# Modulated convolution chain, four layers on one core: the prologue in another order on PE, ACT and DVE

## The reference

```python
def _layer(x, style, w, b, mw, mb, typ):
    s = style @ mw.T + mb
    weight = SCALE * w * s[:, None, :, None]
    demod = lax.rsqrt(jnp.sum(weight * weight, axis=(2, 3)) + EPS)
    weight = weight * demod[:, :, None, None]
    if typ == 'same':
        out = jax.vmap(_conv_same)(x, weight) + b[None, :, None]
    elif typ == 'upsample':
        out = jax.vmap(_conv_up)(x, weight.transpose(0, 2, 1, 3)) + b[None, :, None]
        out = _blur(out, 2.0 * blur_k, (1, 1))
    elif typ == 'downsample':
        xb = _blur(x, blur_k, (2, 2))
        out = jax.vmap(_conv_down)(xb, weight) + b[None, :, None]
    return out
# TYPES = ('same', 'upsample', 'same', 'downsample'); result = x + layer3(layer2(layer1(layer0(x))))
```

## Time and profile before

| | us |
|---|---|
| timed runs: median (lowest to highest of 3) | 169.01 (168.2 to 170.15) |
| the profiled execution's own time | 168.33 |
| its span | 166.5 |
| PE busy in the span | 158.8 (95%) |
| DVE busy | 131.8 (79%) |
| POOL busy | 94.4 (57%) |
| ACT busy | 56.4 (34%) |

### The profile page before, as it was taken

The page is one execution under the profiler, slowest core; times in us unless marked ns, Lnnn a source line. Parts: engine busy times, 40 slices in busy tenths (PEclk is TensorE's granted clock), DMA queues, the critical chain, the costliest instruction groups (busy, mean ns, idle before and its releaser), DMA issues. The chain is left out here.

```text
span 166.5 us, 8946 instructions
## 1 busy us (share of the span) xinstructions
PE 158.8 (95%) x3975; PEld 146.1 (88%) x3975; DVE 131.8 (79%) x229; ACT 56.4 (34%) x127; POOL 94.4 (57%) x155
## 2 busy tenths in 40 slices
PE   7999999999999999999999999999999999999970
PEld 5687888959789789999899999999999999999960
DVE  7859877788868869778696969696979797969993
ACT  3245561323142332334251514243434334231120
POOL 7209908596493977456373829191919192837530
PEclk9959999999999999999999999999999999999998
DMA  4982000120302204335343445353634242030314
GB/s 119 274 212 14 2 4 4 55 79 4 125 8 65 68 4 126 130 130 190 105 183 118 182 133 186 129 193 111 213 110 145 88 143 101 7 126 4 132 74 180
DMA packets 13990, 17.81 MB, mean 107 GB/s; under 512 B 5216, under 2 KB 5760, under 8 KB 13952
## 3 DMA queue, kind: packets, MB, share of 16 engines
q1 hardware_dynamic: 13888, 17.22, 31.1%
q10 hardware_dynamic: 64, 0.02, 0.1%
HBM read 8.85 MB, written 8.39 MB: 104 GB/s over the span
## 5 line engine op out<-in xcount | busy, mean ns | idle before, releaser
L190 POOL TENSOR_TENSOR Hw<-Hw 128x192 f32<-128x192 f32 x15 | 9.0, 598 | 50.8 <-DVE Hw L885 50.8
L546 PE MATMUL p_m<-uu,Hw 64*64 64x128 f32 x992 | 31.6, 269 | 0.0
L546 PEld LDWEIGHTS p_m<-uu,Hw 64*64 64x64 f32 x992 | 29.4, 132 | 0.1
L466 PE MATMUL p_lo<-xin,w0s 64*64 64x259 f32 x384 | 27.7, 406 | 0.1
L309 POOL COPY Hw<-Hw 64x896 f32<-64x896 f32 x15 | 25.8, 1722 | 1.0
L466 PE MATMUL p_le<-xin,w0s 64*64 64x260 f32 x384 | 26.3, 389 | 0.0
L511 PE MATMUL p_le<-R_sb,F_st 64*64 64x128 f32 (+2 forms) x768 | 25.8, 266 | 0.3 <-issue 0.3
L536 PE MATMUL p_m<-u,Hw 64*64 64x256 f32 x384 | 25.4, 375 | 0.0
L896 DVE TENSOR_TENSOR uu<-u 128x516 f32<-128x516 f32 x32 | 24.3, 796 | 1.4
L911 DVE TENSOR_TENSOR e_sb<-p_lo,s_sb 128x512 f32<-128x512 f32 x16 | 11.1, 696 | 16.8 <-PE p_lo L546 16.6
L511 PEld LDWEIGHTS p_le<-R_sb,F_st 64*64 64x64 f32 x768 | 23.3, 133 | 1.1 <-issue 0.9
(11 more groups left out here) (140 smaller groups left out, 217.8 us busy)
## 6 DMA issues: line engine op xcount, KB each, us to landing
xin<-in_x_dram SPq DMA_DIRECT2D x32, 256.0 KB, 3.3
out_dram<-ot SPq DMA_DIRECT2D x32, 256.0 KB, 2.4
wn<-in_L_cond_weights_dram SPq DMA_DIRECT2D x1, 192.0 KB, 3.5
mwn<-in_L_cond_mod_w_dram SPq DMA_DIRECT2D x1, 128.0 KB, 2.2
xe<-in_x_dram SPq DMA_DIRECT2D x2, 56.0 KB, 7.7
cn<-in_cond_dram ACTq DMA_DIRECT2D x1, 16.0 KB, 2.0
bn<-in_L_cond_mod_b_dram ACTq DMA_DIRECT2D x1, 1.0 KB
bn<-in_L_cond_biases_dram ACTq DMA_DIRECT2D x1, 1.0 KB
```

Of the source, the lines that this page charges most:

```text
L466: ins = pe.matmul(bank[h * C:(h + 1) * C, s, 0:n], w0s[p % 2][rows, k, :], xin[p % NX][rows, i0:i0 + 2 * n - 1:2], start=(k == 0), stop=(k ...
L546: ins = pe.matmul(bank(h)[s * C:(s + 1) * C], tap(p, h, s, blk), moving(slice(h * C, (h + 1) * C), s, k), start=(k == 0), stop=(k == len(b ...
```

## The change

The warm-up of PE and its tile are removed. Layer 0 of pair 0 is started as soon as its scaled weights are there; the transposes of wsum stand after its first tap, in p_le instead of p_lo, and the demodulation matmuls after its second.

The diff, cut to its core:

```diff
@@ PE @@
-            pe.wait_ge(warm_made, 1)
-            for _ in range(4):
-                pe.matmul(p_le[:, 1, 0:256], pe_warm[:, 0:P], pe_warm[:], start=True, stop=True)
...
-            layer0_odd(0)
+            pe.wait_ge(w0s_made, 1)
+            pe.wait_ge(x_loaded[0], 32)
+            layer0(0, p_lo, NO, 1, lo_done, [0])
+            pe.wait_ge(made["wsum"], 1)
+            for l in range(LAYERS):
+                ins = pe.transpose(p_le[0:C, 0, l * C:(l + 1) * C], wsum[:, l, :], ident[0:C, 0:C])
+            ins.then_inc(put["wsumT"], 1)
+            layer0(0, p_lo, NO, 1, lo_done, [1])
+            pe.wait_ge(copied["wsumT"], 1)
+            pe.wait_ge(made["style2"], 1)
...
+            ins.then_inc(put["demod"], 1)
+            layer0(0, p_lo, NO, 1, lo_done, [2])
             layer0(0, p_le, NE, 0, le_done)
-            pe.wait_ge(copied["V_st"], 2)
-            compose_R(0)
...
             blurred_taps(1, p_m2[:, 1], cid2, NF).then_inc(put["FT"], 1)
+            pe.wait_ge(copied["V_st"], 2)
+            compose_R(0)
+            pe.wait_ge(copied["G_mv"], 1)
+            blurred_taps(3, b_m13[1], cid1, 3).then_inc(put["oT"], 1)
+            pe.wait_ge(copied["F_st"], 1)
+            compose_H(0)
             taps_transposed(2, b_m13[0], 256).then_inc(put["w2T"], 1)
+            compose_R(1)
...
-            compose_H(0)
-            compose_R(1)
-            blurred_taps(3, b_m13[1], cid1, 3).then_inc(put["oT"], 1)
@@ ACT @@
-            act.wait_ge(put["wsumT"], 1)
-            copy(wsumT[:], p_lo[0:C, 0, 0:LAYERS * C].rearrange("p (l c) -> p l c", c=C), copied["wsumT"])
...
             copy_both(G_mv, p_m13[0:C, 1, 0, 0:K * C].rearrange("p (a c) -> p a c", c=C), copied["G_mv"])
+            act.wait_ge(put["wsumT"], 1)
+            copy(wsumT[:], p_le[0:C, 0, 0:LAYERS * C].rearrange("p (l c) -> p l c", c=C), copied["wsumT"])
...
+            evac_odd(0)
             act.wait_ge(made["e2"], 1)
...
             make_A(0)
-            evac_odd(0)
-            act.wait_ge(made["e1"], 1)
-            evac_R(0)
             act.wait_ge(put["FT"], 1)
...
+            act.wait_ge(made["e1"], 1)
+            evac_R(0)
             make_A(1)
...
@@ DVE @@
-            dve.memset(pe_warm[:], 0.0).then_inc(warm_made, 1)
...
-            then()
-            step(dve.tensor_reduce(wsum[:], wsq[:], AX_X, ALU.add), "wsum")
...
-            tt(style2[:], style[0:C], style[0:C], ALU.mult, "style2")
             ts(pvec[0:C, W_S0], style[0:C, 0, 0:B:2], 1.0)
             ts(pvec[C:P, W_S0], style[C:P, 0, 1:B:2], 1.0, name="s0")
+            step(dve.tensor_reduce(wsum[:], wsq[:], AX_X, ALU.add), "wsum")
+            tt(style2[:], style[0:C], style[0:C], ALU.mult, "style2")
...
+            make_diffs(0)
             demodulation(0, 2)
-            make_diffs(0)
...
-            make_uu(0)
-            demodulation(3, 4)
...
+            demodulation(3, 4)
...
             edge_x0()
+            make_uu(0)
             dve.wait_ge(put["oc"], 1)
```

More of the change, by code:

```diff
@@ L87, in modulated_conv_kernel @@
         sqrt_warm = sb("sqrt_warm", [P, 1])
-        pe_warm = sb("pe_warm", [P, 256])
         y_st = sb("y_st", [P, 6, C])
@@ L130, in modulated_conv_kernel @@
         padded = sem("padded")
-        warm_made = sem("warm_made")
         zeroed = sem("zeroed")
@@ L440, in _ @@
             taps_transposed(0, b_m13[0], 0).then_inc(put["w0T"], 1)
[L442 to L445, removed]
             for a in range(K):
@@ L450, in _, with layer0 @@
             ins.then_inc(put["GT"], 1)
[L452 to L461, removed]
+            def layer0(p, bank, n, first, done, ks=range(K)):
+                for k in ks:
                     for s in range(2):
@@ L468, in layer0 @@
                                             stop=(k == K - 1), skip_group_check=True)
-                ins.then_inc(done, 1)
+                if ks[-1] == K - 1:
+                    ins.then_inc(done, 1)
             def layer0_odd(p):
@@ L629, in edge_out @@
                 ins.then_inc(put["oe"], 1)
-            layer0_odd(0)
+            pe.wait_ge(w0s_made, 1)
[8 more added lines that the diff above has]
+            pe.wait_ge(made["style2"], 1)
+            for l in range(LAYERS):
+                ins = pe.matmul(p_m2[0:C, 0, 256 + l * B:256 + (l + 1) * B], wsumT[:, l], style2[:, l, :],
+                                start=True, stop=True)
+            ins.then_inc(put["demod"], 1)
+            layer0(0, p_lo, NO, 1, lo_done, [2])
             layer0(0, p_le, NE, 0, le_done)
-            pe.wait_ge(copied["V_st"], 2)
-            compose_R(0)
             pe.wait_ge(made["cid"], 1)
@@ L645, in _ @@
             ins.then_inc(put["yc"], 1)
-            pe.wait_ge(copied["F_st"], 1)
-            compose_H(0)
-            compose_R(1)
-            blurred_taps(3, b_m13[1], cid1, 3).then_inc(put["oT"], 1)
             layer0_odd(1)
@@ L772, in _ @@
                            scale=1.0 / 32).then_inc(copied["F_st"], 1)
+            act.wait_ge(made["e1"], 1)
+            evac_R(0)
             make_A(1)
-            act.wait_ge(put["w2T"], 1)
-            copy(w2T[:], p_m13[0:C, 0, 1, 0:3 * C].rearrange("p (k c) -> p k c", c=C), copied["w2T"])
+            act.wait_ge(put["oT"], 1)
+            act.activation(o_st[:], p_m13[:, 1, 0, 0:3 * C].rearrange("p (a c) -> p a c", c=C), ACT.Copy,
+                           scale=0.125).then_inc(copied["o_st"], 1)
             scale_w0(1)
@@ L778, in _ @@
             evac_H(0)
+            act.wait_ge(put["w2T"], 1)
+            copy(w2T[:], p_m13[0:C, 0, 1, 0:3 * C].rearrange("p (k c) -> p k c", c=C), copied["w2T"])
             evac_R(1)
             make_A(2)
-            act.wait_ge(put["oT"], 1)
-            act.activation(o_st[:], p_m13[:, 1, 0, 0:3 * C].rearrange("p (a c) -> p a c", c=C), ACT.Copy,
-                           scale=0.125).then_inc(copied["o_st"], 1)
             evac_odd(1)
```

## The result

| | before | after |
|---|---|---|
| timed runs: median, us (lowest to highest of 20) | 168.6 (167.95 to 170.15) | 170.62 (169.06 to 172.32) |
| the profiled execution's own time, us | 168.33 | 169.27 |
| its span, us | 166.5 | 167.5 |

The changed kernel is slower: ratio 1.0089, 95% interval 1.0061 to 1.0118. (It compares means, 168.75 with 170.26, and leaves out as disturbed three of the 20 runs after, 171.79 to 172.32; with them it would be 1.0105.) The forecast was 169.1, with 167.5 to 170.6 as the range.

The account below looks back on a forecast made before the run. PE was taken to bound the main loop (busy 39.65 of 40 us), so prologue shifts move the end: 168.33 + 0.92 (demodulation) - 0.70 (POOL) + 0.55 (w2) = 169.1 us. The range was 167.5 to 170.6.

Parts of the forecast that it names:

- the mark that I summed for: Start of layer 0 of pair 1 on PE, where the prologue releases the main loop: 21.24 instead of 20.47, +0.77 us.
- the first of the signs that I had set for being wrong: Forecast counts as wrong if PE doesn't wait for POOL inside compose_H(0), where about 1 us was expected.
- Warm-up away: Prologue: saves 3.78 us of PE with little to do; style at 5.9 to 6.5; 0.2 added for lower clock.
- The demodulation late: PE prologue: demodulation, behind wsum's transposes and two layer 0 taps, starts at 9.56 against 8.64, +0.92 us.
- The clock back at 11.9: PE's granted clock rises at 11.9 as before, so layer 0's even half mostly runs at the higher level.
- POOL decides: POOL's chain from e2 shortens by 0.7 to 5.42 us; F's copy ends at 18.48; PE waits about 1.0 us.
- w2 costs 0.55: w2's transposes ahead of compose_R(1) on PE delay R_sb and layer 0 of pair 1 by 0.55 us.
- DVE's other moves cost nothing: Moved differences, demodulation(3,4) (1.0 us, before zc) and uu(0) (1.38 us, behind edge_x0) cost no time.
- A: The case as summed: layer 0 starts early, the demodulation late, POOL's chain ends last; 169.1 us, chance 0.45.
- B: Faster: clock comes back during layer 0's first tap, near 8.5; 167.5 us, chance 0.2.
- C: Slower: clock low for another stretch, with PE waiting before the last third of compose_H(0); 170.7 us, chance 0.15.
- D: Slower on DVE: uu(0)'s two operations each wait for a POOL copy of place_H(1); 170.2 us, chance 0.1.

Follow-up runs that it names:

- b_nowarm: Kernel before without the four PE warm-up matmuls and their tile, order otherwise untouched: 166.92 us, ratio 0.9916 to before.
- a_warm: Changed kernel with the four warm-up matmuls and their tile put back: 171.59 us, ratio 1.0169 to before.
- a_head: Changed kernel with layer 0 whole behind the demodulation, and demodulation(3,4), w2's transposes and the first steps in old order: 167.21 us, ratio 0.9917 to before.
- a_poolfree: Changed kernel without POOL's wait for e2 ahead of prod: 170.56 us, ratio 1.0134 to before.
- b_uu: Kernel before with make_uu(0) moved behind edge_x0 on DVE: 168.08 us, ratio 0.9987 to before.
- a_w2_d34: Changed kernel with demodulation(3,4) back ahead of the first block sum and w2's transposes and copy back at their old places: 168.56 us, ratio 1.0014 to before.
- b_nowarm_uu: Kernel before without the warm-up and with make_uu(0) behind edge_x0: 167.11 us, ratio 0.9925 to before.
- a_nosplit: Changed kernel with layer 0 of pair 0 in one piece behind wsum's transposes and the demodulation: 171.12 us, ratio 1.0122 to before.

## Why the prediction was right or wrong

The direction of the change at the mark that I summed for, and the end, were right: layer 0 of pair 1 at 21.46 against 21.24, the profiled time 169.27 against 169.1, and the loss within 1%. But the median, 170.62, lies at the upper end of my range, and the loss of 0.89%, 1.5 us, is about twice the 0.77 us that I forecast. The way there was right only in part, and it failed at the first of the signs that I had set for being wrong: PE doesn't wait for POOL inside compose_H(0). That 21.24 came close is luck. PE reached compose_H(0) at 17.96, 1.7 later than my 16.3: 0.9 of it is the even half at the lower level, 0.5 the demodulation and the taps around it. That took the place of the wait of 1.0 for POOL, which isn't there, and of 0.3 that I gave w2 too much.

- **Warm-up away.** style at 5.9 to 6.5 held (5.96 to 6.56), and layer 0's early start nearly (7.75 against 7.45). What failed is the judgement of the edit as a whole: it is a gain of 0.84%, and so hides that the rest of the change costs twice what the result shows. I never summed what the edit does alone. The 0.2 for the lower level was also too small: the groups of 0.65 and 0.74 take 1.06 and 0.90. The Trainium skill (TensorE: Matmul & The Clock Gate, "Why this matters for your kernels") names warming up with matmuls first as the way to benchmark matmul accurately. It doesn't say that a warm-up pays inside a kernel, and in this one it doesn't: b_nowarm (0.9916) and a_warm against after (+0.8%). The load of mod_w lands here before the warm-up ends.
- **The demodulation late.** Right in kind, too small: the start was 10.31 and not 9.56, dt +1.62 and not +0.92 (11.35; 9.73 before, one row behind the demodulation's start). I gave a tap 0.88 in issue and the transposes 0.35. The rows have 1.08 and 0.56 (7.75 to 8.83 to 9.39), and 0.92 for the second tap. For the transposes the level explains it, not the dense work around them: they take the same 0.56 in b_nowarm (6.99 to 7.55) among small matmuls, and I had their price from the earlier trace rows, where the level was the higher one. Also, I took wsum behind s0 for free. Its time was nearly right (ready at 7.94; I had 7.85), and in after PE doesn't wait for it; but a_head shows that with layer 0 in one piece the order of the first steps is worth 0.88%.
- **The clock back at 11.9.** Wrong by 2.8 us: 14.66. This is the step that was mis-sized most. The even half took 2.60 in issue (11.84 to 14.44), not 1.7 (11.3 to 13.0), so the F taps started at 14.44.
- **POOL decides.** The price was right in kind, and somewhat too small: copies of 0.28 and 0.34, prod's start to the end of the copy 5.04 against 6.04 before. The wait was wrong: with PE late by itself, at 17.96 instead of 16.3, the 1 us isn't there, and a_poolfree shows that an earlier copy brings nothing. The Trainium skill's rule on the port (SBUF — State Buffer, "SBUF: two separate sides") agrees with both copies in after and in b_uu. It also fits DVE's 0.65 and 0.67 for two operations on Hw at 22.25 and 22.82: POOL's z_st and xse run beside them (20.59 to 23.40), and each took 0.21 before. a_w2_d34 bears it out: with POOL done at 21.92 they take 0.22 each.
- **w2 costs 0.55.** From compose_H(0) to layer 0 of pair 1 it was 3.28 (17.19 to 20.47) and is 3.50: 0.22. In time, a_w2_d34 finds 0.1% or nothing once demodulation(3,4) is back.
- **DVE's other moves cost nothing.** Wrong, and the larger miss in the mechanism. demodulation(3,4) didn't "fall into the time before zc", since the block sum was itself late and slower (the two operations above): zc came at 26.48 and PE waited 0.68. I had looked at the cover of uu(0), which is in fact free (b_uu), and not at this one.
- **The rivals.** A, the one I summed, came near in its time and fell with the wait for POOL. B (clock back during the first tap) didn't happen. C came true in its mechanism, but at another wait than I named: not at compose_H(0), but at zc, and by the mean clocks in about a third of the runs. D didn't happen: a late uu(0) is free (b_nowarm_uu). The DVE row that PE waited for was zc at 26.48, just ahead of the 27 to 30 that I watched.

The profile shows the shift of +1.83 at 27.51 melt to +0.9 in the loop. Measured at the even half of layer 0, from pair 1 (behind the fall of the clock, where there is one) to pair 10, it falls in the profiles of all the other kernels as well, by 0.3 to 1.3. So it belongs to before, to its one profiled execution or to the kernel; these profiles can't tell which. Idle time of PE explains little of it. The waits of PE from 28 to 164 us (tile, line, what ended them, us in total, times, the longest) of before:

```profile
PE p_le L511 <- issue: 0.3, 1, 0.3
```

and of a_nosplit:

```profile
PE p_m L528 <- issue: 1.1, 2, 0.8
```

What those are stays open. They mean that two single profiles can't be compared at the end of the span to better than about a microsecond; my 169.1, made against one, hit 169.27 of another, while the medians are 2 us apart. That, too, is luck.

## What to carry to other kernels

A warm-up is to be weighed against the first work that stands behind it on its engine: if its matmuls end after that work's load has landed, leave it out and measure. Starting the large work early is worth nothing when a small chain behind it (here the reduction, the transposes, the demodulation, e2) sets the next step: order the first operations by which chain the next large step waits for, here the reduction ahead of the scales. Each move of a few short operations on a vector engine needs its own cover checked against the late case, and a short wait of PE among small matmuls has to be priced with a chance of the clock falling behind it.
